# First self attention of a decoder: scores as one pass over high and low parts on 64 rows a head, rows placed by DMA, sine part swapped by DMA

## The reference

```python
q = (X @ W_Q + b_Q)      # 64 heads of 16: 4 branches x 16
k_base, v_base = X @ W_K + b_K, X @ W_V + b_V      # 16 heads, used by all 4 branches
q, k = _rope(q), _rope(k)      # even and odd features turned by cos and sin of the position
scores = einsum('bhtd,bhsd->bhts', q, k) / 4
w = softplus(scores / sqrt(clip(sum(k * k), 1e-6)))
w = where(causal, w, 0);  w = w * sigmoid(SCALE * w);  w = where(w < sinks, 0, w)
out = (w @ v + sinks * v_null) / (sum(w) + sinks + 1e-6)
y = mean over branches of (out @ W_O + W_O_bias)
```

## Time and profile before

| | us |
|---|---|
| median of three runs | 2978.27 (2976.98 to 2987.23) |
| the profiled execution | 2978.33 |
| its span | 2976.5 |
| the first attention in it | 30.4 to 842 |
| PE busy in the span | 2667.9 |
| mean granted clock | 0.933 |

### The profile page before, as it was taken

The page is one execution under the profiler, slowest core; times in us unless marked ns, Lnnn a source line. Parts: engine busy times, 40 slices in busy tenths (PEclk is TensorE's granted clock), DMA queues, the critical chain, the costliest instruction groups (busy, mean ns, idle before and its releaser), DMA issues. The chain is left out here.

```text
span 2976.5 us, 49262 instructions
## 1 busy us (share of the span) xinstructions
PE 2667.9 (90%) x18536; PEld 2086.4 (70%) x18536; DVE 1781.1 (60%) x4040; ACT 1560.2 (52%) x3054; POOL 801.8 (27%) x889
## 2 busy tenths in 40 slices
PE   5999999999866899999979999999969999859998
PEld 4556656565455567677669888989957777648887
DVE  3567665675447556665456666767765656454444
ACT  2777666776534344444445565656546656542221
POOL 1133222232111344444521111111006656600000
PEclk8799998998678899999989999999989999979999
DMA  3000000000012111111010000000020000020000
GB/s 114 5 4 5 5 1 4 5 5 1 1 47 75 32 45 27 26 26 28 22 43 4 6 6 6 3 1 1 1 73 5 8 5 5 1 100 8 8 8 29
DMA packets 88763, 59.42 MB, mean 20 GB/s; under 512 B 55120, under 2 KB 78416, under 8 KB 88016
## 3 DMA queue, kind: packets, MB, share of 16 engines
q1 hardware_dynamic: 88528, 56.25, 6.4%
HBM read 39.46 MB, written 8.39 MB: 16 GB/s over the span
## 5 line engine op out<-in xcount | busy, mean ns | idle before, releaser
L685 DVE SCALAR_TENSOR_TENSOR a_w<-a_w,a_sinks 128x384 f32<-128x384 f32 x512 | 348.5, 734 | 124.3 <-ACT a_w L510 123.9
L2034 POOL TENSOR_SCALAR x_weights<-x_weights,x_sums 128x256 f32<-128x256 f32 x256 | 232.5, 928 | 271.8 <-DVE x_sums L2093 271.8
L1124 POOL TENSOR_SCALAR f_weights<-f_weights,f_sums 128x256 f32<-128x256 f32 x256 | 232.7, 928 | 267.9 <-DVE f_sums L1354 267.9
L338 PE MATMUL psum<-a_qT,a_kT_half 32*128 32x512 f32 x768 | 244.0, 720 | 21.7 <-ACT a_w L491 19.6
L491 ACT ACTIVATE a_w<-psum 128x1024 f32<-128x1024 f32 x192 | 188.1, 1024 | 132.5 <-PE psum L343 132.1
L343 PE MATMUL psum<-a_future,a_unit 32*128 32x128 f32 (+5 forms) x1536 | 238.7, 436 | 0.0
L1282 ACT ACTIVATE f_weights<-psum,f_negmax 128x256 f32<-128x256 f32 x256 | 117.9, 473 | 210.1 <-DVE f_negmax L1348 210.1
L343 PEld LDWEIGHTS psum<-a_future,a_unit 32*128 32x128 f32 x1536 | 136.6, 215 | 111.1 <-issue 110.2
L1619 ACT ACTIVATE a_turned_w_hi<-psum 128x512 fp32r<-128x512 f32 x256 | 139.1, 596 | 142.5 <-PE psum L1529 142.4
L2004 ACT ACTIVATE x_weights<-x_masked_s,x_negmax 128x256 f32<-128x256 f32 x256 | 127.0, 497 | 137.1 <-DVE x_negmax L2085 137.1
L1736 DVE TENSOR_REDUCE a_negmax<-psum 128x1 f32<-128x1024 f32 x128 | 156.6, 1224 | 55.7 <-PE psum L119 51.4
(11 more groups left out here) (357 smaller groups left out, 7402.1 us busy)
## 6 DMA issues: line engine op xcount, KB each, us to landing
f_xnT<-all_xnT_all SPq DMA_DIRECT2D x16, 256.0 KB, 2.4
f_pv_rows<-f_pv SPq DMA_DIRECT2D x8, 512.0 KB, 3.2
f_pv_groups<-f_pv_rows SPq DMA_DIRECT2D x8, 512.0 KB
f_w<-in_f_w SPq DMA_DIRECT2D x2, 2048.0 KB, 10.3
all_x_all<-in_x SPq DMA_DIRECT2D x1, 2048.0 KB, 8.5
a_xnT<-all_xnT_all SPq DMA_DIRECT2D x8, 256.0 KB, 2.3
x_xnT<-all_xnT_all SPq DMA_DIRECT2D x8, 256.0 KB, 2.3
x_ctxT<-in_x_ctxT SPq DMA_DIRECT2D x8, 256.0 KB, 3.0
```

The costliest lines, as they stand in the source:

```text
L338: pe.matmul(psum[:, 2 * x + h, :], kT_half[rows[h], step % 2, g, keys], queries, start=True, stop=False)
L685: ins = dve.scalar_tensor_tensor(part, part, sinks[:, col:col + 1], part, ALU.is_ge, ALU.mult)
L1124: ins = pool.tensor_scalar(w, w, sums[:, k, h, t:t + 1], None, ALU.mult)
L2034: ins = pool.tensor_scalar(w, w, sums[:, k, h, t:t + 1], None, ALU.mult)
```

## The change

Queries and keys are split in a high part, rounded to float32r, and the rest. Four copies of each feature's row (queries high, high, low, low; keys high, low, high, low) make 64 rows a head, and one score product in float32r over them gives the sum of all four part products; both heads of a pair fill 128 rows. The mask comes in two halves of 64 rows: four mask products a slot instead of eight. Queries are projected once, a quad (4 heads x 4 branches) at a time, all 256 keys at once; the swapped weights are gone. For the sine part DVE multiplies the plain projection by cos (`by_cos`) and by sin (`by_sin`), and SP moves `by_sin` one row up or down by two DMAs (`turned_sin`). POOL adds `by_cos` and `turned_sin` twice (rounded and not) and takes the difference, and SP places the parts by 16 DMAs a quad (32 rows of 2 KB each) in `q_rows`, by 16 DMAs for each half of the keys (32 rows of 1 KB each) in `k_rows`. SP's order in a batch is: queries of quad 2; of quad 3; the swap of the next batch's keys; queries of its quad 0, then placing of its keys' first half; queries of its quad 1, then the second half. The output product is cut in two items, one for each half of the tokens, and `ctxT` holds one half. `WINDOW`, `BEHIND` and the order on DVE (`TAKEN_AFTER`) are new; the first window item goes ahead of the half sum. The copy of x for the values is gone. The weights `wks`, `wqs` (0.25 and 1 MB) and half of the mask table (0.25 MB) are no longer loaded.

```diff
-WINDOW = {0: [("regroup", 3, OLD), ("q", 0, HERE), ("q", 1, HERE), ("q", 2, HERE), ("q", 3, HERE)],
-          2: [("k", 0, AHEAD), ("k", 1, AHEAD), ("v", 0, HERE), ("regroup", 6, OLD)],
-          4: [("q", 0, AHEAD), ("q", 1, AHEAD), ("q", 2, AHEAD), ("regroup", 0, HERE)],
-          6: [("q", 3, AHEAD), ("out", 0, OLD), ("regroup", 1, HERE)]}
-
-BEHIND = {0: [("regroup", 4, OLD)], 1: [("regroup", 5, OLD)], 2: [("regroup", 7, OLD)], 3: [("norm", 0, AHEAD)],
-          4: [("turn", 0, OLD), ("turn", 1, OLD)], 5: [("turn", 2, OLD), ("turn", 3, OLD)], 6: [], 7: [("regroup", 2, HERE)]}
-
-WINDOW_AFTER = {0: (0, 1, 2, 3, 4), 2: (0, 1, 2, 3), 4: (0, 1, 2, 3), 6: (0, 6, 7)}
-BEHIND_AFTER = 5
+WINDOW = {0: [("q", 2, HERE), ("regroup", 4, OLD)],
+          2: [("q", 3, HERE), ("v", 0, HERE), ("regroup", 6, OLD)],
+          4: [("q", 0, AHEAD), ("norm", 0, AHEAD), ("out", 0, OLD), ("regroup", 0, HERE)],
+          6: [("q", 1, AHEAD), ("out", 1, OLD), ("regroup", 2, HERE)]}
+
+BEHIND = {0: [("regroup", 5, OLD)], 1: [], 2: [("regroup", 7, OLD), ("k", 0, AHEAD)], 3: [("turn", 0, OLD), ("turn", 1, OLD)],
+          4: [("regroup", 1, HERE), ("turn", 2, OLD), ("turn", 3, OLD)], 5: [], 6: [("regroup", 3, HERE)], 7: []}
+
+TAKEN_AFTER = {0: {("q", 2): -1, ("regroup", 4): 1, ("regroup", 5): 5},
+               2: {("q", 3): -1, ("v", 0): 0, ("regroup", 6): 1, ("regroup", 7): 5, ("k", 0): 6},
+               4: {("q", 0): -1, ("norm", 0): 0, ("out", 0): 3, ("regroup", 0): 3, ("regroup", 1): 5},
+               6: {("q", 1): -1, ("out", 1): 2, ("regroup", 2): 3, ("regroup", 3): 5}}
 
...
         def _(sp):
-            for b in range(B):
-
-                wait(sp, v_done, b)
-                sp.dma_start(xnT[:], xnT_all[:, bass.ds(b, 1), :, :]).then_inc(v_x_here, 16)
+            def swap(r):
+
+                sp.wait_ge(rot_made, r + 1)
+                for to in range(2):
+                    sp.dma_start(turned_sin[to:P:2], by_sin[1 - to:P:2]).then_inc(swapped, 16)
+
+            def place_queries(n):
+
+                sp.wait_ge(q_split, n + 1)
+                wait(sp, scored, (n - 1) * 2 * SLOTS)
+                for part in range(PARTS):
+                    for high in range(2):
+                        for pair in range(2):
+                            lo = 64 * high + 32 * pair
+                            sp.dma_start(q_rows[part:P:PARTS, n % 2, pair, 2 * high:2 * high + 2, :].bitcast(F32),
+                                         q_parts[lo:lo + 32, part // 2, :, :].bitcast(F32)).then_inc(q_here[n % 2], 16)
+
+            def place_keys(bb, c):
+
+                if c == 0:
+                    sp.wait_ge(k_split, bb + 1)
+                wait(sp, scored, ((bb - 1) * 2 + c + 1) * PAIRS_OF_HEADS * SLOTS // 2)
+                for part in range(PARTS):
+                    for pair in range(4):
+                        lo = 32 * pair
+                        sp.dma_start(k_rows[part:P:PARTS, 4 * c + pair, :].bitcast(F32),
+                                     k_parts[lo:lo + 32, part % 2, c, :].bitcast(F32)).then_inc(k_here[c], 16)
+
+            def body(b, new, ahead, old):
+                for step, kind, i in ((0, "q", 2), (2, "q", 3), (2, "k", 0), (4, "q", 0), (6, "q", 1)):
+                    if new if (step, kind) in ((0, "q"), (2, "q")) else ahead:
+                        swap(rotations(b, kind, i))
+                        if kind == "q":
+                            place_queries((b + (step >= 4)) * QUADS + i)
+                        if step >= 4:
+                            place_keys(b + 1, i)
+
+            over_batches(sp, body)
 
...
-                n, g = bb * PAIRS_OF_HEADS + step, step // 4
+                n, g, quad = bb * PAIRS_OF_HEADS + step, step // 4, bb * QUADS + step // 2
                 if x == 0 and step % 4 == 0:
-                    pe.wait_ge(kheads_ready, bb * 2 + g + 1)
-                    pe.wait_ge(rotated, bb * ROTATED + 6 + 4 * g)
+                    pe.wait_ge(k_here[g], (bb + 1) * MOVES)
+                if x == 0 and step % 2 == 0:
+                    pe.wait_ge(q_here[quad % 2], (quad // 2 + 1) * MOVES)
 
                 if not isinstance(n, int) or n > 0:
                     pe.wait_ge(plus_done, (n - 1) * SLOTS + x + 1)
-                heads = [4 * (step // 2) + step % 2 + 2 * h for h in range(2)]
-                rows = [slice(32 * (u % 8 // 2), 32 * (u % 8 // 2) + 32) for u in heads]
+                rows = [slice(64 * h, 64 * h + 64) for h in range(2)]
                 branches = 2 if x < 2 else BR
                 for h in range(2):
-                    keys, queries = (slice(0, P), qT[rows[h], g, 2 * x:2 * x + 2, :]) if x < 2 else \
-                        (slice(P, T), qT[rows[h], g, :, P:T])
-                    pe.matmul(psum[:, 2 * x + h, :], kT_half[rows[h], step % 2, g, keys], queries, start=True, stop=False)
-                for c in range(4):
-                    until = 32 * (c + 1)
+                    of_quad = q_rows[rows[h], quad % 2, step % 2]
+                    keys, queries = (slice(0, P), of_quad[:, 2 * x:2 * x + 2, :]) if x < 2 else (slice(P, T), of_quad[:, :, P:T])
+                    pe.matmul(psum[:, 2 * x + h, :], k_rows[rows[h], step, keys], queries, start=True, stop=False)
+                for c in range(2):
+                    until = 64 * (c + 1)
                     for h in range(2):
                         to = psum[:, 2 * x + h, :].rearrange("p (r t) -> p r t", r=branches)[:, :, 0:until]
                         ins = pe.matmul(to, unit[rows[h], c, :],
-                                        future[rows[h], c, 0:until].unsqueeze(1).to_broadcast([32, branches, until]),
-                                        start=False, stop=(c == 3))
+                                        future[rows[h], c, 0:until].unsqueeze(1).to_broadcast([64, branches, until]),
+                                        start=False, stop=(c == 1))
                 ins.then_inc(scored, 1)
 
...
                     if kind in "qk":
-                        g = 0 if when == AHEAD else 1
-                        lo = i * P if kind == "k" else (2 * i + g) * P
-                        for v, weights in enumerate((wk, wks) if kind == "k" else (wq, wqs)):
+                        weights = wk if kind == "k" else wq
+                        for part in range(2):
+                            lo = ((0 if kind == "k" else 2 * i) + part) * P
                             for c in range(CC):
-                                ins = pe.matmul(spare[:, v * T:(v + 1) * T], weights[:, c, lo:lo + P],
-                                                xnT_all[:, bass.ds(bb, 1), c, :], start=(c == 0), stop=(c == CC - 1))
+                                ins = pe.matmul(spare[:, part * T:(part + 1) * T], weights[:, c, lo:lo + P],
+                                                xnT_all[:, bb, c, :], start=(c == 0), stop=(c == CC - 1))
                         ins.then_inc(projected, 1)
                     elif kind == "v":
-                        pe.wait_ge(v_x_here, bb * 16 + 16)
                         for t in range(TT):
                             for c in range(CC):
-                                ins = pe.matmul(spare[:, t * D:(t + 1) * D], xnT[:, c, t * P:(t + 1) * P], wv[:, c, :],
+                                ins = pe.matmul(spare[:, t * D:(t + 1) * D], xnT_all[:, bb, c, t * P:(t + 1) * P], wv[:, c, :],
                                                 start=(c == 0), stop=(c == CC - 1))
                         ins.then_inc(v_done, 1)
...
-                        pe.wait_ge(turn_taken, bb * 4 + 4)
-                        for t in range(TT):
-                            for k in range(8):
-                                ins = pe.matmul(spare[:, t * D:(t + 1) * D], ctxT[:, t, k, :], wo[:, k, :],
-                                                start=(k == 0), stop=(k == 7))
+                        pe.wait_ge(turn_taken, bb * 4 + 2 * i + 2)
+                        for k in range(8):
+                            ins = pe.matmul(spare[:, 0:D], ctxT[:, k, :], wo[:, k, :], start=(k == 0), stop=(k == 7))
                         ins.then_inc(out_done, 1)
 
...
                         next_scores(step, 0)
+                        send_all(WINDOW[step][:1], step)
                         quad = quad_at(b, step // 2 - 2, new, old)
                         if quad:
                             sum_half(b, quad, 1, spare_bank(b, step, "sum", 1))
-                        send_all(WINDOW[step], step)
+                        send_all(WINDOW[step][1:], step)
...
-                    act.activation(ctxT[:, i // 2, 4 * (i % 2):4 * (i % 2) + 4, :],
+                    wait(act, out_done, (b - 1) * TT + i // 2)
+                    act.activation(ctxT[:, 4 * (i % 2):4 * (i % 2) + 4, :],
                                    spare.rearrange("p (k n) -> p k n", k=4), ACT.Copy).then_inc(turn_taken, 1)
 
...
+                def split_queries(n, r):
+
```

(78 more changed lines are left out.)

183 lines of the change are left out of this document (70 added, 113 removed).

## The result

The changed kernel takes 3028.93 us (median of four runs, 3024.76 to 3037.22) against 2977.62 us of the kernel before (2975.93 to 2987.23) beside it: a ratio of 1.0169, 95% interval 1.0137 to 1.0201. It is slower by 1.7%, where 2911 us, 2.3% less, was forecast. The profiled execution took 3024.76 us, its span is 3023.0 us, its mean granted clock 0.907 (0.933 before).

A forecast was written before the change was run, and what follows sets the result against it. TensorE bounded the kernel before; ACT would come next. 74 + 4 + 4 = 82 us a batch, 10.8 less, eight times: 2978.3 - 86.4 + 19 = 2911 us; range 2838 to 3004, the forecast's own 2862 to 2960.

The forecast's parts named there:

- the chain queue by queue: SP's serial queue of swaps and placings: 0.42 us an issue, 70.7 us a batch, barely below ACT's 74.
- The second rival: SP's queue sets the pace, at 0.59 us an issue or with POOL's divisions before the splits: 2973 us; chance 0.13.
- the third of my signs: A sign that the forecast is wrong: DVE waiting long for POOL ahead of the rotations.
- TensorE: Score slots with 64-row pairs side by side: 0.50 and 0.65 us each; PE falls to some 57 us a batch.
- What comes next: ACT, +4, +4: ACT alone needs 74 us a batch, plus 4 for its wait behind late keys and 4 for TensorE's clock: 82 us.
- The clock: TensorE falls to its low clock in one and a half of four quads, 2.8 us each: 4 us a batch.
- 3018 us: Rival: TensorE's low clock holds in every quad's scores, 95 us a batch, slower; chance 0.19.
- The late keys: Key swap and POOL's sum end late, holding up PE, so ACT waits: 4 us a batch, between 0 and 8.
- The start: First projection to first score takes 34.2 us, not 22.4; with earlier loads and late query quads, 19 us lost in all.

## Why the prediction was wrong

**The step that failed** is in the chain queue by queue: "I take 0.42, the two rows nearest in shape. That fits below ACT's 74, barely." The price was 0.63 us an issue, start to start, and more in some rows: 62.7 us for the 96 placing issues of a batch instead of 40.3. I had taken it from sixteen loads in a row from DRAM, 8 KB each, which the runs show not to be the nearest: an 8 KB DMA from SBUF to SBUF costs the same 0.63 as one of 64 KB. The upper bound of 0.59, from one load, was too low as well, if barely: one placing issue behind another lasts 0.60 us (the one at 440.44), and it and the next together 1.23. Two rows of the kernel before went unread or were misread. Its trace has a copy from SBUF to SBUF, 256 KB:

```profile
857.71 0.47 SPq L758 DMA_DIRECT2D x_xnT<-all_xnT_all  x1
```

With 0.47 the sum for SP is 70.7 + 4.8 = 75.5 us, above ACT's 74 already. (It is issued after a rest; the placing issue at 439.90, the first after a rest, lasts 0.50 us too.) The 128 KB of the earlier trace rows, which the sum takes to go from SBUF to SBUF, are a store to DRAM (`mix_rows` is a DRAM tensor); that the swap lands in 2.0 us as that store does in 1.9 is luck. With the measured 62.7 us in place of 40.3 my own sum gives SP 70.7 + 22.4 = 93 us a batch, no gain over the kernel before. The rest of that sum held: the four gaps were 25.3 us (1 us of them for TensorE) where I had 4 x (1.9 + 4.6) = 26; swaps took 6 us instead of 4.5; and 4.6 us of waiting for DVE that I had not counted closes the loop.

**The second rival** (SP sets the pace) is what happened. I gave it 0.13 and priced it at 89 us a batch; it came to 99. Saying "fits, barely" of a serial queue with waits in its middle, with bounds of 64 (by its own terms 65) to 87 around a limit of 74, should have had a far larger chance. The sign that I gave for it, PE waiting for landed queries, did not come: between 130 and 730 us PE waited for a landing ahead of scores once, 2.3 us. The lateness came out where buffers are given back instead, at DVE's rotations: the third of my signs, which I had not tied to SP.

**TensorE** came out as planned. At the high clock (1.00 from 463 to 470 us) a slot takes 465.44 to 466.00, 0.56 us (0.50 and 0.65 forecast):

```profile
465.44 0.50 PE L382 MATMUL psum<-a_q_rows,a_k_rows 64*128 64x512 f32 x2
465.77 0.39 PE L387 MATMUL psum<-a_future,a_unit 64*128 64x128 f32 x4
466.00 0.42 PE L382 MATMUL psum<-a_q_rows,a_k_rows 64*128 64x512 f32 x2
466.24 0.40 PE L387 MATMUL psum<-a_future,a_unit 64*128 64x128 f32 x4
```

PE is busy 59.3 us a batch in the kernel that places through DRAM, where I had 57 to 65. The pairs on 64 rows do run side by side: the two score products of a slot take 466.24 - 466.00 = 0.24 us, where a single product of 512 columns took 0.23.

**What comes next: ACT, +4, +4** could be tested once SP was out of the way: 78 us a batch, where I had 74 + 4 + 4 = 82, within the forecast's own 76 to 88. The total of that part was sound; its three terms, and that ACT is what sets it, no run took apart.

**The clock** does swing more: 0.78 in the stretch against 0.90. The Trainium skill, "TensorE: Matmul & The Clock Gate", section "A second HAM failure mode: psum-queue depth-cycling", describes this for a TensorE that often idles between groups, and the trace agrees with the swing. But from it I had 3018 us, close to the 3029 measured and for the wrong reason: with twice the score products the clock is higher and the time is the same, and with SP freed the clock is 0.87 and the batch 78 us. (The low level in all quads was my reading; the section speaks of swings.)

**The late keys** do wait: in the kernel through DRAM DVE's rotations wait for POOL's key sum 27.0 us in seven batches, 3.9 us each; in the changed kernel it is 82.1 us between 130 and 730 us, because the swap that POOL waits for is late. The 4 us that I charged were for ACT, and how much of DVE's wait reaches ACT no run shows.

**The start** took 39.7 us from first projection to first score against the 34.2 forecast. Two placings of 10.05 us instead of 6.7 are 6.7 us, a little more than the whole miss. The projection began at 26.67 instead of 30.36, 3.7 us earlier (4.5 forecast). Of the whole 51 us, seven batches at 6.8 us more make 47; the first value projection comes 17.8 us later, and the stretch from the last one to the end of the stage is 16 us shorter.

## What to carry to other kernels

Count the DMAs that a queue issues in the loop and price each as one fixed time, measured on the very kind of DMA in steady issue; where no such row exists, the sum has to hold at the dearest price on record. Then add every landing and every other engine's work that the queue waits for between them. When such a sum comes near the next engine's time, it is the likeliest bound, not a rival. The cure here was fewer, larger DMAs, even by way of DRAM: 106 a batch became 44, and the same change went from 1.7% slower to 4.3% faster. Issuing from a second queue was not tried.

## What the runs showed that I had not expected

- A placing DMA from SBUF to SBUF behind another one costs SP 0.63 us, independent of bytes (8, 32, 64 KB), rows (16, 32) and spread. The Trainium skill, "Perfetto Trace Analysis", section "What "DMA-bound" means", says that where the issuing queue is solid with DMA slices, large descriptors are what matters. Here SP issued for 68.7 of 98.6 us. The runs agree that the queue can be the bound, and not that the descriptor counts: rows of 256 bytes and of 2 KB took the same, and only the number of DMAs moved the time. Why the sixteen loads of the earlier trace rows took 0.36 to 0.47 us each, I did not find; a source in DRAM is not enough, since the four loads of 256 KB took 0.70 us each.
- The granted clock went up when TensorE was given more to do (0.78 to 0.82, and 0.87 to 0.90), and the batch grew by far less (0.7 and 1.4 us) than the work added (4 us a batch).
- DVE's threshold, untouched by the change, takes 734 ns before, 768 in the changed kernel and 853 through DRAM, where the same work is packed into shorter batches. Which neighbour slows it was not tried.

```profile
L734 DVE SCALAR_TENSOR_TENSOR a_w<-a_w,a_sinks 128x384 f32<-128x384 f32 x512 | 406.8, 853 | 12.1 <-ACT a_w L559 12.1
```
